# Last layer of a four-layer network: grouped norm shifts, a reordered spread, four identity sums and row-tiled FFN matmuls

## The chip, the cores and the metric

One core of a Trainium2 chip runs the kernel. The metric is the device time of one execution in microseconds (us), the median of several runs. Engines are named as in the profile: PE is TensorE's matmuls, PEld its weight loads, DVE is VectorE, ACT is ScalarE, POOL is GpSimd, SP is SyncE, which issues the DMAs.

## The reference

The input is x of shape (4, 32, 16, 16): 4 images, 32 channels, 256 pixels. Four layers run one after another, each as `x = x + layer(group_norm(x))`: a 7x7 dynamic filter, a deformable 3x3 convolution, twenty row and column updates, and the last layer, the only one that the change touches:

```
# last layer, x normalised, patches = 9 reflected 3x3 shifts of x
counts  = 1 + round(7 * (df - dmin) / (dmax - dmin + 1e-8))   # df = |laplacian(mean_c x)|
kvals   = minimum(counts, 9)
sim     = <x, patch_k> / (|x| * |patch_k|)                    # 9 per pixel
order   = argsort(-sim);  wts = exp(sim) where rank < kvals, else 0
out     = sum_k wts_k * patch_k / sum_k wts_k
enhanced = out + group_norm(x, weight, bias, 16 groups)
h       = relu(w1 @ enhanced + b1)                            # 32 -> 64 channels
return enhanced + w2 @ h + b2                                 # 64 -> 32 channels
```

## The kernel before

Partition 32b+c holds channel c of image b, so a tile is 128 partitions x 256 pixels. There is no loop over tiles: everything is written out by hand, and each engine runs its own list in order, with semaphores between them. `HALVES` are pixels 0 to 127 and 128 to 255. PSUM is one tensor `ps` of 8 banks x 512 floats. The last layer starts when the third layer's result is turned back (L1023 to L1031) and `x3` is made (L752).

**Norms and similarities.** ACT copies the normalised image to `g3c` (L555) and squares it into `maps[0]` (L557). PE makes the channel means (L1069), the squared norms of 324 padded pixels by one matmul with a 4-column weight (L1073), the Laplacian (L1078), and four maps of shifted dot products (L1084). ACT copies the norms three times, for the three column shifts, to `norms0`, all on partitions 0 to 3 (L562). PE transposes 3 column shifts x 3 row shifts x 2 halves of them, 18 transposes of 4 x 128 (L1093). ACT copies the dots (L565) and then takes the square root of the transposed norms (L567). DVE makes reciprocals of the norm products and `sim` (L786 to L802), and compares (L806, L808).

**Counts and ranks.** After the Laplacian DVE finds its largest and smallest value (L776 to L783). POOL makes the counts in three instructions, L439, L440 and L441, the last of which writes `kn` in bf16. PE adds up the ranks in bank 6: a constant (L1118), 16 matmuls of the comparisons (L1111), and two of `kn`, in bf16 (L1128). DVE turns rank and `exp(sim)` into weights `wf` (L821). `keep_warm` (L862) puts matmuls of zeros into PE's list, with counts from `WARM`.

**Spread and sum.** PE transposes `wf` (L1135), ACT and DVE copy it to `wrows`. `spread3(c)` (L1138) copies the weights of one column shift c to all channels: three matmuls of 32 rows, each into its own bank. DVE multiplies with the patches, three at a time (L837), giving `prod3[c]`, `prod3[3+c]`, `prod3[6+c]`. The third spread reuses the banks of the first, so it waits for the first product. The inverse weight sums `rden` are turned (L1157), copied (L576), spread (L1161) and copied to `rb` (L578). Six matmuls with the identity add the terms in bank 0 (L1167): some are products, some are pairs that POOL (L452) or DVE (L841) has added before.

**FFN.** `wc` holds w1 and w2 as block matrices of 128 x 128, two for each layer. Blocks off the pairs are zero. `normed` (L1148) puts w1 times the group-normed image into the hidden banks, L1189 adds w1 times `enh` (L845). ACT and DVE make the ReLU (L581, L849), L1194 multiplies with w2, accumulating two blocks, L854 adds bias and residual, and SP stores each half (L350). f32 matmuls are two records each in the profile, f32 transposes one.

POOL's list also has a stretch of fills and constant building (L414 to L429), between the second layer and its part of the third layer's moves, which wait for `g2` (L431 to L435).

Of the kernel before, what the change touches and what calls it, by code (L numbers as in the profile page):

```python
# [19 lines left out]
BF16 = mybir.dt.bfloat16  # L20
ALU = mybir.AluOpType
ACT = mybir.ActivationFunctionType
# [3 lines left out]
P = B * C  # L26
# [46 lines left out]
WARM = (9, 23, 12, 14, 5, 1, 2)  # L73
# [18 lines left out]

SHIFTS = (1, PAD - 1, PAD, PAD + 1)
# [23 lines left out]
def build(nc, x_d, par_d, ident_d, taps_d, wconv_d, wa_d, wb_d, wc_d, cst_d, sel_d, sel0_d, cb_d, out_d):  # L117
    with ExitStack() as ctx:
# [71 lines left out]
        norms0 = sb("norms0", [B, 3, PAD * W])  # L190
# [6 lines left out]
        kn = sb("kn", [B, HW], BF16)  # L197
# [9 lines left out]
        rden = sb("rden", [P, LINES, Q])  # L207
        wrows = sb("wrows", [P, HW])
        rrows = sb("rrows", [P, HW])
        rb = sb("rb", [P, HW])  # L210
        sum3 = sb("sum3", [P, 3, HW])
# [142 lines left out]
        def _(g):  # L354
# [104 lines left out]
        def _(a):  # L459
# [107 lines left out]
            a.activation(nn[:, :, :, :].rearrange("p l k b -> p (l k b)"), ps[:, 0, 0:LINES * KB],  # L567
                         ACT.Sqrt).then_inc(nn_ready, 1)
# [7 lines left out]
            a.activation(rrows[3 * Q:P, :], ps[3 * Q:P, 1, HW:2 * HW], ACT.Copy).then_inc(rrows_ready, 1)  # L576
            a.wait_ge(r_spread, 1)
            a.activation(rb[:, :], ps[:, 1, 0:HW], ACT.Copy).then_inc(rb_ready, 1)  # L578
            for n, pixels in enumerate(HALVES):
                a.wait_ge(h_done, 2 * n + 1)  # L580
# [4 lines left out]
        def _(v):  # L585
# [210 lines left out]
            v.tensor_tensor(some_k(sim, 4, 1), view(ps[:, 0, 4 * B:4 * B + 1], (KB, LINES), (B, 1), (1, B)),  # L796
# [7 lines left out]
            v.wait_ge(fills_ready, 3)  # L804
# [28 lines left out]
            v.reciprocal(rden[:, :, 0:B], den[:, :].rearrange("p (l b) -> p l b", b=B)).then_inc(rden_ready, 1)  # L833
# [7 lines left out]
            v.tensor_tensor(sum3[:, 2, :], prod3[:, 5, :], prod3[:, 8, :], ALU.add).then_inc(sum_v, 1)  # L841
# [461 lines left out]
```

## Time and profile before

| | us |
|---|---|
| median of 3 runs | 110.9 |
| lowest, highest | 110.66, 111.75 |
| profiled execution, its device time | 111.37 |
| its span, first to last instruction | 109.3 |
| PE busy in the span | 95.5 |
| DVE busy | 71.8 |
| ACT busy | 52.0 |
| POOL busy | 29.4 |

The span is 2.1 us shorter than the execution's time; what lies around it is start and end of the program. The profile page gives busy times, the clock granted to TensorE, and the chain of work that ended last. The timeline gives instructions in order of time, with the idle time of their engine before them and what ended it. Matmuls are pipelined, so their busy times overlap and start-to-start distances say more. Times in the text are from the span's start.

### The profile page before, as it was taken

What the parts mean: (1) busy time and instruction counts of PE and PEld (TensorE: products, weight loads), DVE (VectorE), ACT (ScalarE), POOL (GpSimd) and SP (SyncE); (2) the same over time, 40 slices, a digit from 0 to 9 for tenths busy, and PEclk for the clock granted to TensorE, in tenths of its full rate; (3) what the DMA queues carried; (4) which work ended last, traced back from release to release, by engine and by line L of the source; (5) the groups of instructions that cost most, each with busy time, mean ns of one, the idle gap of its engine ahead of it and who ended that gap; (6) DMA issues with size and microseconds to landing.
All of it is one profiled execution on the core that took longest, in us unless ns stands there. A gap on an engine that the chain in (4) does not pass through costs nothing.

```text
span 109.3 us, 2956 instructions
## 1 busy us (share of the span) xinstructions
PE 95.5 (87%) x1209; PEld 68.8 (63%) x1213; DVE 71.8 (66%) x201; ACT 52.0 (48%) x107; POOL 29.4 (27%) x43
## 2 busy tenths in 40 slices
PE   5959997596775999999967999999999899888990
PEld 2336642394555777777732899979998644554990
DVE  4653988139999998398437655565555669667542
ACT  5643826215999999757424999000000045621120
POOL 3000821790000003999972000000000000763130
PEclk9999999999999999999999999999999999999999
DMA  2899999999100000000000000000000000000001
GB/s 72 212 342 375 196 188 199 193 191 219 31 0 0 6 0 3 0 6 0 6 13 0 0 0 6 0 6 0 6 0 6 0 3 6 0 0 0 0 0 48
DMA packets 4684, 6.37 MB, mean 58 GB/s; under 512 B 560, under 2 KB 3936, under 8 KB 4672
## 3 DMA queue, kind: packets, MB, share of 16 engines
q1 hardware_dynamic: 4672, 6.20, 25.0%
q8 instruction: 9, 0.15, 0.6%
q14 instruction: 3, 0.02, 0.1%
HBM read 6.07 MB, written 0.13 MB: 57 GB/s over the span
## 4 chain that ended last, share of the span: by engine, by line
PE 69%; DVE 16%; ACT 5%; DMA 4%; issue 2%; SPq 1%; DVEq 0%
PE ps L1055 22%; PE ps L982 13%; PE ps L993 8%; PE ps L882 5%; DMA taps<-in_taps 4%; PE ps L862 3%; DVE st L698 3%; PE ps L1167 3%; PE ps L934 2%; DVE g1x L660 2%; DVE yt L734 2%; PE ps L919 1%; ACT s L532 1%; PE ps L1141 1%; PE ps L1189 1%
## 5 line engine op out<-in xcount | busy, mean ns | idle before, releaser
L698 DVE TENSOR_TENSOR st<-hats 128x1024 f32<-128x1024 f32 (+1 forms) x21 | 20.9, 1043 | 2.2 <-PE ps L982 2.2
L982 PE MATMUL ps<-ident,st 128*128 128x128 f32 x144 | 17.9, 277 | 2.4 <-DVE st L698 2.4
L532 ACT ACTIVATE s<-ps 128x512 f32<-128x512 f32 x33 | 17.3, 601 | 4.5 <-PE ps L982 4.5
L982 PEld LDWEIGHTS ps<-ident,st 128*128 128x128 f32 x144 | 15.6, 141 | 6.0 <-DVE st L698 3.5
L862 PE MATMUL ps<-zeros 128*128 128x512 bf16 x62 | 16.3, 409 | 2.4 <-DVE zeros L607 1.2
L1055 PE MATMUL ps<-yt,wband 128*64 128x96 f32 (+1 forms) x240 | 12.5, 260 | 0.8 <-DVE yt L734 0.8
L463 ACT ACTIVATE std<-mv,par 128x1 f32<-128x1 f32 x4 | 1.2, 295 | 24.6 <-DVE mv L595 24.6
L862 PEld LDWEIGHTS ps<-zeros 128*128 128x128 bf16 x66 | 6.6, 105 | 9.9 <-issue 1.9
L1055 PEld LDWEIGHTS ps<-yt,wband 128*64 128x64 f32 x240 | 11.5, 136 | 2.2 <-issue 1.2
L1055 PE MATMUL ps<-ytb,wband 128*64 128x96 f32 (+1 forms) x240 | 12.2, 259 | 0.1
L1055 PEld LDWEIGHTS ps<-ytb,wband 128*64 128x64 f32 x240 | 11.3, 136 | 0.9 <-DVE ytb L748 0.2
L741 DVE SCALAR_TENSOR_TENSOR ytb<-ps,ytb 128x64 f32<-128x64 f32 (+7 forms) x36 | 6.9, 228 | 5.4 <-PE ps L1055 5.4
L741 DVE SCALAR_TENSOR_TENSOR yt<-ps,yt 128x64 f32<-128x64 f32 (+7 forms) x36 | 6.9, 228 | 5.3 <-PE ps L1055 5.3
L993 PE MATMUL ps<-s,mixed 128*32 128x256 f32 x144 | 9.5, 385 | 0.9 <-ACT s L532 0.9
L439 POOL TENSOR_SCALAR df<-df,mm 4x256 f32<-4x256 f32 x1 | 1.2, 1220 | 33.6 <-DVE mm L783 33.6
L400 POOL TENSOR_TENSOR st<-hats 128x1024 f32<-128x1024 f32 x1 | 2.9, 2947 | 18.3 <-PE ps L982 18.3
L882 PE MATMUL ps<-taps,g0t 128*128 128x352 f32 (+1 forms) x20 | 5.9, 433 | 1.3 <-DMA taps<-in_taps 1.3
L410 POOL TENSOR_SCALAR wband<-wband 128x384 f32<-128x384 f32 x4 | 6.8, 1732 | 0.2 <-POOL st L400 0.2
L548 ACT ACTIVATE wband<-wband 128x384 f32<-128x384 f32 x16 | 6.7, 508 | 0.0
L993 PEld LDWEIGHTS ps<-s,mixed 128*32 128x32 f32 x144 | 3.8, 109 | 4.1 <-ACT s L532 1.1
L882 PEld LDWEIGHTS ps<-taps,g0t 128*128 128x128 f32 x20 | 3.5, 190 | 3.1 <-issue 1.8
L488 ACT ACTIVATE hid<-ps 128x512 f32<-128x512 f32 x4 | 2.2, 598 | 3.3 <-PE ps L893 3.3
(180 smaller groups left out, 128.8 us busy)
## 6 DMA issues: line engine op xcount, KB each, us to landing
wband<-in_wb SPq DMA_DIRECT2D x4, 720.0 KB, 15.8
wa<-in_wa SPq DMA_DIRECT2D x1, 576.0 KB, 8.3
taps<-in_taps SPq DMA_DIRECT2D x1, 560.0 KB, 5.9
taps<-in_taps SPq DMA_DIRECT2D x1, 448.0 KB, 4.8
wa<-in_wa SPq DMA_DIRECT2D x1, 324.0 KB, 5.8
wc<-in_wc SPq DMA_DIRECT2D x1, 256.0 KB, 14.9
cst<-in_cst SPq DMA_DIRECT2D x1, 242.0 KB, 6.1
sel<-in_sel SPq DMA_DIRECT2D x1, 192.0 KB, 5.0
```

The lines of the kernel that those rows point to most:

```text
L400: g.tensor_tensor(st[:, k % 2, half, :, :].rearrange("p b (y x) -> p b y x", x=W), view(hats[:, half, k, 0, 0:1], (16, B), (1, H), (0, W)) ...
L410: g.tensor_scalar(wband[:, n, :, :], wband[:, n, :, :], 2.0, None, ALU.mult).then_inc(early_doubled, 1)
L532: a.activation(s[:, k % 2, kb, 2 * pair:2 * pair + 2, :], ps[:, turn_bank(e), :], ACT.Copy).then_inc(drained_a, 1)
L548: a.mul(wband[:, n, :, :], wband[:, n, :, :], 2.0).then_inc(band_doubled, 1)
L698: v.tensor_tensor(st[:, k % 2, half, low:low + count, :].rearrange("p b (y x) -> p b y x", x=W), view(hats[:, half, k, low, 0:1], (16, cou ...
L741: v.scalar_tensor_tensor(out=lanes, in0=view(ps[:, Z_BANKS[n >= STEPS // 2][pair], frm:frm + 1], (H, 8), (1, count)), scalar=0.0, in1=lane ...
L862: t.matmul(ps[:, bank, :], zeros[:, 0:P], zeros[:, :], start=True, stop=True)
L882: last = t.matmul(out[:, :, y0:y0 + ROWS7, :], g0t[:, half, :], taps7[:, 2 * i:2 * i + n, lo:lo + ROWS7, :], start=(half == 0), stop=(half ...
L982: last = t.transpose(ps[:, turn_bank(e), HW * i + P * half:HW * i + P * half + P], st[:, k % 2, half, 2 * pair + i, P * kb:P * kb + P], id ...
L993: last = t.matmul(ps[Q * b:Q * b + Q, 0, 0:HW], mixed[:, kb, col:col + C], s[:, k % 2, kb, b, :], start=(k == 0 and kb == 0), stop=(k == T ...
L1055: last = t.matmul(ps[low:low + 64, Z_BANKS[n >= STEPS // 2][pair], 0:2 * LANE].rearrange("p (b n) -> p b n", b=2)[:, :, H * to:H * (to + c ...
L1167: return t.matmul(ps[:, 0, 0:HW], ident[:, :], term, start=first, stop=last)
```

## The change

It touches only the last layer and POOL's fills for it.

- The norms' weight becomes `norm3`, 96 columns wide, so that the squared norms come out on partitions 0 to 3, 32 to 35 and 64 to 67, and each column shift goes to a group of its own. Six transposes of 68 x 128 take the place of 18 of 4 x 128. The square root reads 12 of each 68 columns.
- POOL fills `norms0` and `norm3`, makes three small copies and `neg`, and no longer fills `rden`.
- `kn` is f32, and its matmul uses `neg`, in f32 too. The constant of the ranks (L1118) moves ahead of the `keep_warm` in front of the comparisons, behind a wait for `mm_ready`.
- One matmul of zeros fewer before the spreads. The wait for `lapw_ready` moves ahead.
- `rden` is turned by two transposes onto partitions 0 to 3. `spread3(2)` is issued ahead of the wait for `rrows` and the spread of the inverse sums.
- The sums: POOL adds a third (`sum3[1] + prod3[7]`), DVE a second (`prod3[2] + prod3[5]`, then `+ prod3[8]`). Four identity matmuls remain of six.
- FFN: each 128 x 128 matmul pair becomes four matmuls on the nonzero blocks, 32 rows x 64 columns for w1, 64 rows x 32 columns for w2.

```diff
-WARM = (9, 23, 12, 14, 5, 1, 2)
+WARM = (9, 23, 12, 14, 5, 1, 1)
+NT_ROWS = 2 * Q + B
...
# POOL
-            g.memset(rden[:, :, :], 0.0).then_inc(fills_ready, 1)
             g.memset(sim[:, LINES * KB:], 0.0).then_inc(fills_ready, 1)
+            g.memset(norms0[:, :], 0.0).then_inc(fills_ready, 1)
+            step(g.memset(norm3[:, :], 0.0))
+            for dx in range(3):
+                g.tensor_copy(norm3[:, Q * dx:Q * dx + B], cst[:, C_NORM:C_NORM + B]).then_inc(fills_ready, 1)
             step(g.memset(lapw[:, :], 0.0))
             g.wait_ge(ident_loaded, 16)
+            g.wait_ge(fills_ready, 6)
+            step(g.tensor_scalar(neg[:, :], ident[0:B, 0:B], -1.0, None, ALU.mult))
...
+            g.wait_ge(sum_g, 2)
+            g.tensor_tensor(sum3[:, 3, :], sum3[:, 1, :], prod3[:, 7, :], ALU.add).then_inc(sum_g, 1)
# ACT
             for dx in range(3):
-                a.activation(norms0[:, dx, :].rearrange("p (h w) -> p h w", w=W),
-                             view(ps[0:B, 7, dx:dx + 1], (PAD, PAD), (1, W)), ACT.Copy).then_inc(norms0_ready, 1)
+                group = slice(Q * dx, Q * dx + B)
+                a.activation(norms0[group, :].rearrange("p (h w) -> p h w", w=W),
+                             view(ps[group, 7, dx:dx + 1], (PAD, PAD), (1, W)), ACT.Copy).then_inc(norms0_ready, 1)
...
-            a.activation(rrows[3 * Q:P, :], ps[3 * Q:P, 1, HW:2 * HW], ACT.Copy).then_inc(rrows_ready, 1)
+            a.activation(rrows[:, :], ps[0:B, 1, HW:2 * HW], ACT.Copy).then_inc(rrows_ready, 1)
...
# DVE
-            v.tensor_tensor(sum3[:, 2, :], prod3[:, 5, :], prod3[:, 8, :], ALU.add).then_inc(sum_v, 1)
+            v.tensor_tensor(sum3[:, 4, :], prod3[:, 2, :], prod3[:, 5, :], ALU.add).then_inc(sum_v, 1)
+            v.wait_ge(sum_v, 1)
+            v.tensor_tensor(sum3[:, 2, :], sum3[:, 4, :], prod3[:, 8, :], ALU.add).then_inc(sum_v, 1)
...
# PE
-            t.matmul(ps[0:B, 7, 0:PAD * PAD], cst[:, C_NORM:C_NORM + B], maps[:, 0, :], start=True,
+            t.matmul(ps[0:3 * Q, 7, 0:PAD * PAD], norm3[:, :], maps[:, 0, :], start=True,
...
-            for dx in range(3):
-                t.wait_ge(norms0_ready, dx + 1)
+            t.wait_ge(norms0_ready, 3)
+            for half in range(2):
                 for dy in range(3):
-                    for half in range(2):
-                        at, frm = KB * half + B * (3 * dy + dx), P * half + W * dy
-                        last = t.transpose(ps[:, 0, at:at + B], norms0[:, dx, frm:frm + P], ident[0:B, 0:B])
+                    at, frm = NT_ROWS * (3 * half + dy), P * half + W * dy
+                    last = t.transpose(ps[:, 0, at:at + NT_ROWS], norms0[0:NT_ROWS, frm:frm + P],
+                                       ident[0:NT_ROWS, 0:NT_ROWS])
...
-                                view(cb[0:B, CB_NEG:CB_NEG + 1], (0, KNN), (1, B)),
+                                view(neg[:, 0:1], (0, KNN), (1, B)),
...
+            def hidden(n, image, first):
+                for b in range(B):
+                    i, j = b // 2, b % 2
+                    last = t.matmul(ps[64 * j:64 * j + 64, H_BANKS[n][i], 0:P],
+                                    wc[C * b:C * b + C, P * i + 64 * j:P * i + 64 * j + 64], image[C * b:C * b + C, HALVES[n]],
+                                    start=first, stop=not first, skip_group_check=True)
+                return last
...
             for half in range(2):
-                last = t.matmul(ps[3 * Q:P, 1, HW + LINE * half:HW + LINE * half + LINE], rden[:, half, :],
-                                ident[:, :], start=True, stop=True)
+                last = t.transpose(ps[0:B, 1, HW + LINE * half:HW + LINE * half + LINE], rden[:, half, :], ident[:, :])
             last.then_inc(rden_turned, 1)
-            t.wait_ge(rrows_ready, 1)
-            t.matmul(ps[:, 1, 0:HW], sel[3 * Q:P, 0:P], rrows[3 * Q:P, :], start=True, stop=True).then_inc(r_spread, 1)
             t.wait_ge(p3_ready, 1)
             spread3(2)
+            t.wait_ge(rrows_ready, 1)
+            t.matmul(ps[:, 1, 0:HW], sel[0:B, 0:P], rrows[:, :], start=True, stop=True).then_inc(r_spread, 1)
...
             add3(sum3[:, 0, :])
+            t.wait_ge(gnout_ready, 1)
             t.wait_ge(p3_ready, 2)
-            add3(prod3[:, 7, :])
-            t.wait_ge(sum_g, 2)
-            add3(sum3[:, 1, :])
-            t.wait_ge(p3_ready, 3)
-            add3(prod3[:, 2, :])
...
+            hidden(0, gnout, True)
+            t.wait_ge(sum_g, 3)
+            add3(sum3[:, 3, :])
+            t.wait_ge(sum_v, 2)
             add3(sum3[:, 2, :], last=True).then_inc(acc3_done, 1)
             t.wait_ge(rb_ready, 1)
-            normed(1, 0)
-            normed(1, 1)
+            hidden(1, gnout, True)
             for n, pixels in enumerate(HALVES):
                 t.wait_ge(enh_ready, n + 1)
...
+                hidden(n, enh, False).then_inc(h_done, 1)
             for n, pixels in enumerate(HALVES):
...
+                t.wait_ge(h_a, n + 1)
+                t.wait_ge(h_v, n + 1)
+                for b in range(B):
+                    i, j = b // 2, b % 2
+                    last = t.matmul(ps[C * b:C * b + C, Y_BANKS[n], 0:P],
+                                    wc[64 * j:64 * j + 64, P * (2 + i) + C * b:P * (2 + i) + C * b + C],
+                                    hff[64 * j:64 * j + 64, i, pixels], start=True, stop=True)
                 last.then_inc(ffn_done, 1)
```

`H_BANKS` is ((5, 6), (7, 1)) and `Y_BANKS` is (2, 3), so in `hidden` two 32-row tiles write one bank, on different partitions, and in the last matmuls all four 64-row tiles write one bank, on different partitions.

## Rows read from the trace of the kernel before

**Rows 1.** The profile page: TensorE's granted clock, in 40 slices of the span

```profile
PEclk9999999999999999999999999999999999999999
```

**Rows 2.** Timeline, 89 to 94: start, duration, engine, line, out<-in, count, [idle before <-releaser]

```profile
89.80 0.61 PE L1069 MATMUL ps<-cst,g3c 128*128 128x4 f32 x4
...
90.34 0.71 PE L1073 MATMUL ps<-maps,cst 128*4 128x324 f32 x2
...
92.39 1.06 PEld L1093 LDWEIGHTS ps<-ident,norms 4*128 4x128 f32 x16 [0.86 <-ACT norms L562]
...
92.50 0.60 ACT L565 ACTIVATE dots<-ps 128x512 f32<-128x512 f32 x1 [0.43 <-PE ps L1084]
...
93.70 0.23 ACT L567 ACTIVATE nn<-ps 128x72 f32<-128x72 f32 x1 [0.61 <-PE ps L1093]
```

**Rows 3.** Timeline, 93 to 97: the counts on POOL, and the ranks

```profile
93.29 1.22 POOL L439 TENSOR_SCALAR df<-df,mm 4x256 f32<-4x256 f32 x1 [33.55 <-DVE mm L783]
...
94.59 0.40 POOL L440 TENSOR_SCALAR df<-df 4x256 f32<-4x256 f32 x1
95.07 1.06 POOL L441 TENSOR_SCALAR kn<-df 4x256 bf16<-4x256 f32 x1
...
96.01 0.20 PE L1118 MATMUL ps<-cb 1*128 1x72 bf16 x1 [0.69 <-DVE above L806]
...
96.64 0.21 PE L1128 MATMUL ps<-cb,kn 4*128 4x36 bf16 x2
...
96.96 0.30 DVE L821 SCALAR_TENSOR_TENSOR wf<-ps,ex 128x36 f32<-128x36 f32 x2 [0.54 <-PE ps L1128]
```

**Rows 4.** Timeline of POOL, 45 to 60

```profile
53.77 0.53 POOL L420 TENSOR_SCALAR lapw<-ident 128x128 f32<-128x128 f32 x1
...
59.12 0.62 POOL L435 COPY yt<-g 32x64 f32<-32x64 f32 x2 [2.14 <-DVE g L604]
```

**Rows 5.** Timeline of DVE, 56 to 58

```profile
56.64 0.63 DVE L725 TENSOR_TENSOR x<-x,r 128x256 f32<-128x256 f32 x1 [1.80 <-ACT r L535]
```

**Rows 6.** Timeline, 97.6 to 103: spreads, products, sums

```profile
97.68 0.29 DVE L826 COPY wrows<-ps 128x128 f32<-128x128 f32 x1 [0.43 <-PE ps L1135]
...
98.12 1.14 PE L1141 MATMUL ps<-wrows,sel 32*128 32x256 f32 x12
...
98.88 1.82 DVE L837 TENSOR_TENSOR prod<-ps,g3p 128x768 f32<-128x768 f32 x2 [0.42 <-PE ps L1141]
...
99.19 0.62 PE L1157 MATMUL ps<-ident,rden 128*32 128x128 f32 x4
...
99.91 1.59 POOL L452 TENSOR_TENSOR sum<-prod 128x256 f32<-128x256 f32 x2 [2.02 <-DVE prod L837]
...
101.09 0.96 DVE L837 TENSOR_TENSOR prod<-ps,g3p 128x768 f32<-128x768 f32 x1 [0.39 <-PE ps L1141]
...
102.08 0.42 DVE L841 TENSOR_TENSOR sum<-prod 128x256 f32<-128x256 f32 x1
```

**Rows 7.** The chain of waits in order of time, 101 to 104.3: start, us, what

```profile
101.00 2.35 PE ps L1167 x10
103.35 0.45 PE ps L1148 x4
103.80 0.43 PE ps L1167 x2
```

**Rows 8.** Timeline, 104.3 to the last store

```profile
104.34 0.49 DVE L845 TENSOR_TENSOR enh<-ps,rb 128x128 f32<-128x128 f32 x2 [1.83 <-PE ps L1167]
...
104.68 1.16 PE L1189 MATMUL ps<-enh,wc 128*128 128x128 f32 x8
...
105.68 1.11 PE L1194 MATMUL ps<-hff,wc 128*128 128x128 f32 x8
106.46 0.79 DVE L854 SCALAR_TENSOR_TENSOR y<-ps,par,xe 128x128 f32<-128x128 f32 x2 [0.23 <-PE ps L1194]
106.84 0.85 SPq L350 DMA_DIRECT2D out<-y  x2
```

More of the change, by code:

```diff
@@ L206, in build @@
         den = sb("den", [P, LINES * B])
-        rden = sb("rden", [P, LINES, Q])
+        rden = sb("rden", [P, LINES, B])
         wrows = sb("wrows", [P, HW])
-        rrows = sb("rrows", [P, HW])
+        rrows = sb("rrows", [B, HW])
         rb = sb("rb", [P, HW])
-        sum3 = sb("sum3", [P, 3, HW])
+        sum3 = sb("sum3", [P, 6, HW])
         gn = sb("gn", [P, 12])
@@ L566, in _ @@
             a.wait_ge(norms_turned, 1)
-            a.activation(nn[:, :, :, :].rearrange("p l k b -> p (l k b)"), ps[:, 0, 0:LINES * KB],
-                         ACT.Sqrt).then_inc(nn_ready, 1)
+            a.activation(nn[:, :, :, :].rearrange("p l (y x) b -> p (l y) x b", x=3),
+                         view(ps[:, 0, 0:1], (NT_ROWS, 3 * LINES), (Q, 3), (1, B)), ACT.Sqrt).then_inc(nn_ready, 1)
             a.wait_ge(gn_paired, 1)
@@ L832, in _ @@
             v.wait_ge(v_step, own[0])
-            v.reciprocal(rden[:, :, 0:B], den[:, :].rearrange("p (l b) -> p l b", b=B)).then_inc(rden_ready, 1)
+            v.reciprocal(rden[:, :, :], den[:, :].rearrange("p (l b) -> p l b", b=B)).then_inc(rden_ready, 1)
             for c in range(3):
@@ L1105, in _ @@
                      stop=True).then_inc(gn_paired, 1)
+            t.wait_ge(mm_ready, 1)
+            t.wait_ge(wc_loaded, 32)
+            t.matmul(view(ps[:, 6, 0:1], (KB, LINES), (B, KNN), (1, B)), cb[0:1, CB_ONE:CB_ONE + LINE],
+                     view(cb[0:1, CB_TAP:CB_TAP + 1], (0, LINES), (G, KNN), (1, B)),
+                     start=True, stop=False, skip_group_check=True)
             keep_warm(WARM[4], 1)
@@ L1116, in _ @@
             t.wait_ge(above_ready, 1)
-            t.wait_ge(wc_loaded, 32)
-            t.matmul(view(ps[:, 6, 0:1], (KB, LINES), (B, KNN), (1, B)), cb[0:1, CB_ONE:CB_ONE + LINE],
-                     view(cb[0:1, CB_TAP:CB_TAP + 1], (0, LINES), (G, KNN), (1, B)),
-                     start=True, stop=False, skip_group_check=True)
             for o in range(1, NEAR + 1):
@@ L1144, in spread3 @@
                 last.then_inc(wb_done, 1)
-            def normed(n, i):
-                t.matmul(ps[:, H_BANKS[n][i], 0:P], wc[:, P * i:P * i + P], gnout[:, HALVES[n]], start=True,
-                         stop=False, skip_group_check=True)
+            def hidden(n, image, first):
[5 more added lines that the diff above has]
+                return last
             t.wait_ge(sel_ready, 1)
@@ L1171, in _ @@
             add3(sum3[:, 0, :])
+            t.wait_ge(gnout_ready, 1)
             t.wait_ge(p3_ready, 2)
-            add3(prod3[:, 7, :])
-            t.wait_ge(sum_g, 2)
-            add3(sum3[:, 1, :])
-            t.wait_ge(p3_ready, 3)
-            add3(prod3[:, 2, :])
-            t.wait_ge(gnout_ready, 1)
-            normed(0, 0)
-            normed(0, 1)
-            t.wait_ge(sum_v, 1)
+            hidden(0, gnout, True)
+            t.wait_ge(sum_g, 3)
+            add3(sum3[:, 3, :])
+            t.wait_ge(sum_v, 2)
             add3(sum3[:, 2, :], last=True).then_inc(acc3_done, 1)
             t.wait_ge(rb_ready, 1)
-            normed(1, 0)
-            normed(1, 1)
+            hidden(1, gnout, True)
             for n, pixels in enumerate(HALVES):
                 t.wait_ge(enh_ready, n + 1)
-                for i in range(2):
-                    t.matmul(ps[:, H_BANKS[n][i], 0:P], wc[:, P * i:P * i + P], enh[:, pixels], start=False,
-                             stop=True, skip_group_check=True).then_inc(h_done, 1)
+                hidden(n, enh, False).then_inc(h_done, 1)
             for n, pixels in enumerate(HALVES):
-                for i, ready in ((0, h_a), (1, h_v)):
-                    t.wait_ge(ready, n + 1)
-                    last = t.matmul(ps[:, Y_BANKS[n], 0:P], wc[:, P * (2 + i):P * (3 + i)], hff[:, i, pixels],
-                                    start=(i == 0), stop=(i == 1))
+                t.wait_ge(h_a, n + 1)
[5 more added lines that the diff above has]
+                                    hff[64 * j:64 * j + 64, i, pixels], start=True, stop=True)
                 last.then_inc(ffn_done, 1)
```

16 lines of the change are left out of this document (9 added, 7 removed).

## The prediction

> **What bounds the kernel.** I read the page first, then the chain of waits in order of time, then the timeline of each engine over the last 25 us. The page shows TensorE's clock granted in full in all 40 slices [rows 1], so no term below needs a clock. The chain shows where the last layer's end is made. From 101.00 to 104.23 it is PE alone: ten records of identity matmuls, four of `normed`, two more identity records [rows 7]. DVE had its last sum ready at 102.50 [rows 6] and then waited 1.83 for PE [rows 8]. After that enh, hidden matmuls, ReLU, last matmuls and bias alternate to 107.25, and SP's second store goes out at about 107.28, half of its 0.85 before 107.69 [rows 8]. In front, two paths meet at the ranks: norms, similarities and comparisons, for which PE waited 0.69 [rows 3], and POOL's counts, ready at 95.07 + 1.06 = 96.13 [rows 3]. The second is only 0.5 ahead of the matmul that needs it, at 96.64. This decides what the first part of the change is worth.
>
> **Norms.** The 18 transposes are issued from 92.39; 16 of them make one piece of 1.06, some 0.066 each [rows 2]. Six at 0.07 to 0.11 end near 93.0, where the square root now starts at 93.70. But ACT is copying the dots until 92.50 + 0.60 = 93.10 [rows 2], so the root starts at about 93.12: 0.58 earlier, and so do reciprocals, `sim` and comparisons. The ACT copies keep their size and end before PE is free at 92.39; waiting for all three costs nothing. L1073 with 96 columns runs in the mode of L1069, and the change to 4-column tiles comes one step later, at L1078: I take +0.04 for the Laplacian and what hangs on it, between -0.1 and +0.2. Moving L1118 away takes its lead over the first rank matmul out, between 0 and its 0.20 [rows 3]; I take 0.13, as matmuls overlap. PE would be done with the 16 rank matmuls at 96.64 - 0.58 - 0.13 = 95.93 and could start `kn`.
>
> **Counts.** It can't, since `kn` is not there. What matters is whether an f32 output makes L441 quicker. L440 does the same 256 elements in 0.40, L441 in 1.06, L439 in 1.22 [rows 3]. L439 writes f32 as L440 does and is slow; L420 writes f32, 128 elements, in 0.53 [rows 4]. L440 multiplies and adds; the others subtract first, or multiply alone. So the slow ones go with the operation pair, not with the type, and I leave L441 at 1.06 (bounds 0.40 and 1.06). `kn` is ready at 96.13 + 0.04 = 96.17 and PE starts at about 96.22; a wait costs 0.05 to 0.07 (L452 starts 0.07 behind the first product's end at 98.88 + 0.96 [rows 6]). The matmul is now f32: four passes with 128-column weights and a short moving side, as L1069, 0.61 [rows 2], where bf16 took 0.21 [rows 3]. That ends at 96.83, against 96.85. The gain of 0.58 + 0.13 is worth 0.02 to 0.04 at L821. If L441 took 0.40, ranks would end at 95.93 + 0.61 = 96.54, 0.31 earlier.
>
> The Trainium skill, page GPSIMD Engine Reference, section Engine selection, says that one-input elementwise work on GpSimd is roughly at line rate. By it L441 should go at L440's pace; three rows here do not agree. By the page the sum would be 0.27 lower.
>
> **POOL's fills.** Two fills, three copies of 128x4 and one 4x4 multiply come in, one fill goes. Each copy at most 0.31 (half of L435), the others at most 0.53 (L420): below 2.1 with the fill that goes, and likelier 1.3 to 1.6. The idle time that covers them is 2.14, ended by `g2` [rows 4]; without the cover each 0.1 would cost 0.1 only once POOL's move came behind DVE's moves. Not quite free: POOL now works under DVE's stage around 57. L725 took 0.63 [rows 5] while POOL added too, the same form in L841 0.42 [rows 6]. I take +0.05 (-0.2 to +0.2).
>
> **Fewer zeros, third spread.** The first spread's matmul starts 0.15 behind the end of L826 [rows 6]; that is two waits rather than the zeros, so the dropped one is worth 0 (0 to 0.08). The turning of `rden`, now two single passes of four, still ends before the first product at 98.88 + 0.96 - 0.04 = 99.80. There the third spread starts, at 99.86, and needs 0.76 as the first did (98.12 to 98.88): third product at 100.62 and not 101.09, just when DVE is free of the second. DVE is 0.47 ahead, product done at 101.58. The inverse sums come behind it in the same rows of the array, ready in `rb` near 101.4, before anyone asks.
>
> **Sums.** DVE now makes two: 101.61 + 2 x 0.42 + 0.04 = 102.49, so what it was ahead is spent. POOL: 1.59 for two from 99.87, a wait of 0.08, another 0.73: 102.27. Both now read SBUF twice at the same time, as in L725: 0 to 0.4 more for DVE, 0 to 0.2 for POOL; I take 102.7 and 102.4. PE has two pairs of identity records done by 102.0 and `hidden` by 102.45. The last two pairs start at 102.5 and need 4 x 0.22 and a tail of 0.25: 103.63 where it was 104.23. **Gain 0.60** (0.45 to 0.75).
>
> **FFN in tiles.** From the first half of enh, 104.63, to the last y, 107.25, it is 2.62 now. The spread is the nearest row for tiles of 32 rows: 12 records in 1.14, where L1167 takes 2.35 for 10 of the same 256 columns [rows 6, 7]; three row tiles do run at once. With 128 columns I take 0.45 for a `hidden` and 0.45 for the last matmuls, mode changes included. First half: 0.05 + 0.45 + 0.04 + ReLU 0.37 + 0.05 + 0.45 + 0.12 + 0.35 = 1.88; second half 0.3 behind, 2.2 in all. The stores need 0.42 each on SP, so the second goes out 0.12 later than y would let it. **Gain 0.30** (0 if tiles take what the full matmuls take, 0.50 if they overlap fully). The second `hidden` of `gnout` lies under DVE's enh.
>
> **The sum.** 0.60 + 0.30 - 0.05 = 0.85. The profiled execution took 111.37, with a span of 109.3: that gives 110.5 and a span of 108.4. The median of the runs shown is 110.9; less 0.8, **110.1 us**. Own range of this case 109.7 to 110.6.
>
> **Rivals.**
> *The counts get fast* (0.15). L441 was slow through its bf16 output. L1128's start then hangs on the norms: another 0.27, 109.8 us. For it: L441 is the only one of the three with bf16. Against: L439 and L420.
>
> *Tiles don't pay* (0.13). Each `hidden` and each set of last matmuls costs as much as the full ones with their mode changes, 1.16 and 1.11 for two halves [rows 8]. FFN gain 0, and 0.1 less before the last adds: 110.5 us. The half of the change that shortens the FFN would do nothing.
>
> *Tiles in one bank go one after another* (0.12), the rival on the slow side. In the trace row tiles always write banks of their own (L1141: one bank for each of three), so no row excludes it. `hidden` would take 8 x 0.11 less half, +0.2 in three places on the path; the last matmuls, four tiles in one bank, 8 x 0.11 = 0.88 a half and not 0.22, +0.85 over both with their overlap gone: 110.1 + 1.4 = 111.5 us. It decides from half of this on; 0.85 lost is no change.
>
> The Trainium skill, page PSUM — Partial Sum Buffer, section PSUM bank collisions raise a hardware error, speaks against the change here: different row tiles can't access one PSUM bank at the same time, and software has to see to it. It also tells that different quadrants of one bank went clean for two engines. No row of this trace shows either.
>
> **Chances.** The rest, 0.60, is the forecast: counts bind, tiles run together. The range must hold forecast, fast counts and idle tiles: from 109.4 (all good bounds together reach 109.3) to 110.9. About 1% is what a measurement of this kernel can tell from no change, that is 109.8 and 112.0. Below 109.8 lie a quarter of the forecast and 0.7 of the fast counts: 0.26. Above 112.0, three in ten of the serial case and a little for contention nobody saw: 0.05. Within: 0.69.
>
> **What would show it.** Right: L567 at about 93.1; L441 still 1.06 and PE idle before L1128; L821 at 96.9; third L837 at 100.6 without idle time; last identity record ended by 103.7; y's last end 2.2 behind enh's first. Wrong: L441 near 0.4; L841 pairs beyond 1.3; records of `hidden` at 0.11 or more apart; POOL later than DVE at its moves for the third layer. Wrong altogether if the first 90 us differ by more than 0.3, since only fills were added there.

## The result and the profile after

The changed kernel takes 115.16 us (median of four executions, 114.63 to 115.75). The kernel before, in four executions beside it, took 111.33 (110.66 to 114.89). The ratio is 1.0366, with a 95% interval of 1.0268 to 1.0465. The ratios in this text compare only executions within 1.5% of the fastest of their own kernel, so the one of 114.89 is left out, while all four of the changed kernel count. The forecast was 110.1. The profiled execution took 115.49, its span is 113.2, and its mean granted clock is 0.94.

The page of the changed kernel, slices of a fortieth of the span (2.83 us) each:

```profile
span 113.2 us, 2980 instructions
...
PEclk9999999769999999999999999999999999955559
```

TensorE's clock was granted in full in every slice of before [rows 1]. Here it falls twice: for a while in slices 8 and 9, and for four slices in the last layer. The view by stretches of the same kernel gives the sizes (start:end and length, then busy time and instructions of PE, PEld, DVE, ACT and POOL, then the granted clock, the DMA share and GB/s):

```profile
21.10:24.60 3.50, 3.50 (x60) 3.50 (x62) 0.82 (x1) 0.34 (x1) 2.44 (x3) 0.51 1.09 191
86.00:99.50 13.50, 11.91 (x135) 6.58 (x136) 9.66 (x38) 5.34 (x13) 4.17 (x5) 1.00 0.01 2
99.50:110.00 10.50, 10.36 (x68) 5.87 (x66) 4.76 (x10) 1.34 (x4) 3.04 (x5) 0.51 0.00 0
110.00:113.20 3.20, 0.70 (x16) 0.19 (x10) 0.84 (x3) 0.15 (x1) 0.00 (x0) 1.00 0.14 41
```

From 99.5 to 110.0 the clock is at its lower level, 1.2 GHz, and that is all of spread and sums and the FFN up to its last matmuls, where PE sets the end. The chain of work that ended last in the changed kernel (start, length, engine and line, number of instructions), from the counts on:

```profile
94.23 1.35 POOL df L447
...
95.65 0.40 POOL df L448
...
96.13 1.16 POOL kn L449
...
97.33 0.63 PE ps L1142 x4
...
98.32 0.45 PE ps L1149 x2
...
99.23 1.73 PE ps L1155 x12
...
101.48 1.16 PE ps L1155 x6
...
103.48 2.01 PE ps L1184 x4
105.49 0.63 PE ps L1164 x8
106.13 2.01 PE ps L1184 x4
108.13 1.20 PE ps L1164 x16
```

L1155 is `spread3`, L1184 the identity sum, L1164 `hidden`. The eight identity records come in two groups of 2.01, about 0.50 each, where before had 0.23 [rows 7]. DVE and POOL, which set the time of the sums in the forecast, are nowhere in the chain between the spread and `hidden`.

**Where 4.12 us went.** The two profiled executions differ by 115.49 - 111.37 = 4.12. The last layer's zeros (L875; L862 before) start at 87.63 and not at 86.84: 0.79 came before it, with the early fall at 21.1. From there to the end of the last y it is 111.19 - 87.63 = 23.56 against 107.26 - 86.84 = 20.42, which is 3.14 more. What is left, 0.19, lies behind y and outside the span. So most of the loss lies where the clock was low, and the experiments ask first what the same code takes where it isn't.

### The profile page after: what moved, and what is told of

It reads as the page before. It is cut to its first block, busy times and chain, and to the rows that moved or that the text cites. A ratio compares the mean times of both kernels' runs of the same rounds, so it can differ in the third digit from the quotient of the medians.

```text
span 113.2 us, 2980 instructions
## 1 busy us (share of the span) xinstructions
PE 99.9 (88%) x1216; PEld 69.9 (62%) x1220; DVE 72.8 (64%) x202; ACT 52.1 (46%) x107; POOL 31.3 (28%) x49
## 4 chain that ended last, share of the span: by engine, by line
PE 68%; DVE 14%; ACT 6%; DMA 4%; issue 3%; POOL 3%; SPq 1%; DVEq 0%
PE ps L1068 21%; PE ps L995 12%; PE ps L1006 8%; PE ps L895 5%; PE ps L947 4%; PE ps L1184 4%; DMA taps<-in_taps 4%; DVE st L709 3%; PE ps L875 3%; PE ps L1155 3%; DVE g1x L671 2%; PE ps L1164 2%; ACT yt L554 1%; PE ps L932 1%; ACT s L542 1%
## 5 line engine op out<-in xcount | busy, mean ns | idle before, releaser
L875 PE MATMUL ps<-zeros 128*128 128x512 bf16 x61 | 15.9, 407 | 2.5 <-DVE zeros L618 1.2
L875 PEld LDWEIGHTS ps<-zeros 128*128 128x128 bf16 x65 | 6.3, 103 | 9.9 <-issue 1.9
L947 PE MATMUL ps<-wa,a1x 128*64 128x72 f32 x72 | 4.1, 306 | 0.7 <-ACT a1x L509 0.7
```

Source lines behind the costliest of these rows:

```text
L875: t.matmul(ps[:, bank, :], zeros[:, 0:P], zeros[:, :], start=True, stop=True)
L947: last = t.matmul(ps[low:low + 64, 7, OFFS * half:OFFS * half + OFFS], a1x[:, dx, at + low:at + low + 64], wa[:, col:col + OFFS], start=(d ...
```

## Experiments: the clock

Line numbers in the profiles are each kernel's own. Executions of the kernel before stood beside each; over the three series, each on another chip, there were 71. Only one execution of a run has a trace. What the others did is told by their mean granted clock and their time. By these the clock fell near the end in 19 of the 71 (mean clock under 0.96, 114.67 to 116.15 us): 6 of 25, 7 of 20 and 6 of 26. In 8 it fell only early (mean 0.983 or 0.984, 111.5 to 112.5), and the median of those that kept it is 110.63. "Fell" below means a fall near the end; how many there were is told for each kernel.

**One matmul of zeros given back.** The changed kernel, with one edit:

```diff
-WARM = (9, 23, 12, 14, 5, 1, 1)
+WARM = (9, 23, 12, 14, 5, 1, 2)
```

> The changed kernel with the one matmul of zeros back in front of the spreads. Theory 'zeros': the dropped matmul is what lets TensorE's clock fall to half at 98.9 us in the changed kernel's trace; then the clock stays at 1.0 to the end and the time is 110 to 111 us. Theory 'thin stretch': PE has had too little to do over several us (6 transposes for 18, waits for the counts), one matmul of 0.2 us does not mend it: clock still 0.94 to 0.95, time 114.5 to 115.5. Theory 'late waits' (POOL's contention and the counts cost the time, not the clock): 115 as well, but with a stretch from the ranks to the end as long as now whatever the clock does.

Measured: median 111.11 of ten executions, one of which fell (115.93). Ratio 1.0067 (1.0027 to 1.0106). The profiled execution took 110.66 with a span of 108.2. Its page:

```profile
PEclk9999999999999999999999999999999999999998
```

And its chain, from the matmul of `kn` on:

```profile
95.82 0.63 PE ps L1142 x4
...
96.81 0.44 PE ps L1149 x2
97.24 0.43 PE ps L875 x2
...
97.72 0.73 PE ps L1155 x6
```

The two zeros matmuls (L875 x2) end 0.05 before the spread, which had to wait for `wrows` anyway, and its first six records take 0.73. From the zeros at 86.06 to the end of the last y at 106.03 this is 19.97, against 20.42 before and 23.56 in the changed kernel. So the new work is 0.45 quicker than the old at full clock, and the fall costs 23.56 - 19.97 = 3.59. One matmul that costs nothing by its own time separates four falls in four from one in ten.

**Four more zeros.** The changed kernel with `WARM` at `(9, 23, 12, 14, 6, 2, 2)`, which is three more, and a fourth ahead of the wait for `kn`:

```diff
...
+            keep_warm(1, 1)
...
```

> The changed kernel with four more matmuls of zeros in places where PE waits: one more before the comparisons, one before the wait for kn, one more after the ranks, one more before the spreads. Theory 'thin stretch': the clock holds at 1.0 from the third layer to the end; time 110.0 to 111.5 us. Theory 'zeros' also gives that. Theory 'late waits': no better than 115, since PE's waits get longer, not shorter. If tiles in one bank went one after another, the FFN from the first enh to the last y would still take over 3.5 us at full clock; if they run together, 2.2.

Measured: 111.10, none of ten fell, ratio 1.0055 (1.0014 to 1.0097). Together with the run before it: where the clock is kept, the changed kernel gains nothing over before; it is 0.6% slower. The sections below ask why.

**The same edit in the kernel before.** Only the last number of `WARM`, from 2 to 1:

```diff
-WARM = (9, 23, 12, 14, 5, 1, 2)
+WARM = (9, 23, 12, 14, 5, 1, 1)
```

> The kernel before with only the one matmul of zeros taken away. Theory 'zeros': the clock falls near 99 us here too, time 114 to 115. Theory 'thin stretch': little happens, 110.9 within 0.5, clock 1.0 in most executions.

Measured: 7 of 10 fell (113.45 to 115.27), median 113.71. The three that kept the clock have a median of 110.45 (ratio 0.9988, 0.9933 to 1.0042), so no change is seen there. The kernel before fell in 6 of the 25 executions beside it, and in 19 of all 71. So dropping the matmul makes falls more frequent by itself, with none of the new work around it. Whether it does so less often than in the changed kernel, four and ten executions can't tell. The time it takes is nothing; a fall that it holds off is worth some 4 us.

**The zeros put elsewhere.** The changed kernel, with the extra one in front of the comparisons and not before the spread:

```diff
-WARM = (9, 23, 12, 14, 5, 1, 1)
+WARM = (9, 23, 12, 14, 6, 1, 1)
```

> The changed kernel with one more matmul of zeros, but ahead of the comparisons instead of in front of the spreads (6, 1, 1 for 5, 1, 1). Theory 'amount': how much PE has done over the stretch decides, wherever it is done: clock falls in few executions, as with the zeros back in their place (1 of 10), median near 111.1. Theory 'place': only work in the last stretch before the spreads holds the clock: falls in most executions, median 114 to 115.5.

Measured: three of four fell, median 115.21 (111.27 to 115.96). So far as four executions can tell, one more in the earlier gap doesn't make up for the one that is missing ahead of the spread.

**Full FFN matmuls.** The changed kernel with `hidden` and the last matmuls as before, 128 x 128:

```diff
...
-            hidden(0, gnout, True)
+            normed(0, 0)
+            normed(0, 1)
...
-                hidden(n, enh, False).then_inc(h_done, 1)
+                for i in range(2):
+                    t.matmul(ps[:, H_BANKS[n][i], 0:P], wc[:, P * i:P * i + P], enh[:, pixels], start=False,
+                             stop=True, skip_group_check=True).then_inc(h_done, 1)
```

> The changed kernel with the FFN of before (full 128 x 128 matmuls), all else as changed. If the light tiles of the FFN are what keeps the clock down for 10 us, the clock comes back sooner and the time is under 114. Theory 'thin stretch': the fall at about 99 us is ahead of the FFN, so it stays; with full matmuls at half clock the time is 115 to 117, clock 0.94 to 0.95.

Measured: four of four fell, 115.14. Since all did, its ratio of 1.0386 (1.0316 to 1.0456) holds the fall. The clock was low from 98.5 to 108.7. The light tiles are not what lets it fall.

**What PE did before the fall.** The same 13.5 us, counted from 1.63 before the last layer's zeros, in five kernels. The changed kernel's is the row 86.00:99.50 above. The kernel before:

```profile
85.21:98.71 13.50, 12.32 (x152) 7.15 (x153) 9.32 (x38) 5.23 (x13) 3.96 (x5) 1.00 0.01 2
```

With one given back:

```profile
84.43:97.93 13.50, 12.08 (x136) 6.64 (x137) 9.66 (x38) 5.34 (x13) 4.22 (x5) 1.00 0.01 2
```

Two kernels of the next section, the norms alone, and the last version, with two more zeros and the constant moved:

```profile
85.22:98.72 13.50, 11.96 (x140) 6.57 (x141) 9.79 (x38) 5.35 (x13) 4.23 (x5) 1.00 0.01 2
...
85.13:98.63 13.50, 12.88 (x154) 7.54 (x155) 9.34 (x38) 5.22 (x13) 3.96 (x5) 1.00 0.01 2
```

PE is busy for 11.91 where four of four fell, but for 11.96 in the norms alone, where none of ten did. Then come 12.08 for one of ten, 12.32 for 19 of 71, and 12.88 for none of ten. So how much PE does in these 13.5 us doesn't order the kernels. What orders them better is the number of zeros matmuls right ahead of the spread:

| ahead of the spread | executions that fell |
|---|---|
| one | 4 of 4, 4 of 4 (full FFN), 3 of 4 (moved), 7 of 10 (before, one dropped): 18 of 22 |
| two | 19 of 71 (before), and 11 of 78 in nine kernels of these experiments: 30 of 149 |

Where the fall begins differs too. Five traces hold one near the end, each 10.2 long. In the three with one such matmul it begins 11.8 to 12.0 behind the last layer's zeros (99.6 in the changed kernel), in the spread. In the two that have the norms and ranks of before (the tiles alone and the six fills, both below) it begins 9.2 and 8.9 behind them, at the end of PE's wait ahead of the ranks or within it. The wait in the tiles alone, whose clock is low from 95.9 on:

```profile
95.89 0.24 PE L1118 MATMUL ps<-cb 1*128 1x72 bf16 x1 [0.69 <-DVE above L806]
```

The zeros ahead of the spread come only after that place (97.48 in before, 10.64 behind the last layer's zeros), so they can't hold off a fall there. That fits two weak places, of which the change and the dropped matmul bear on the second; no run shows it by itself. The kernel before keeps or loses the clock with one and the same list, so what decides in a single execution isn't shown either.

The Trainium skill, page TensorE: Matmul & The Clock Gate, section A second HAM failure mode: psum-queue depth-cycling, tells of a kernel in which the engine idles shortly but often between groups of matmuls, and the clock goes up and down between its two levels. The trace agrees in part: the fall at 99.6 comes behind 1.6 us of idle time (13.50 - 11.91) in short pieces, none of them over 0.3. But the norms alone have 1.5 there and kept the clock in ten of ten, and before has 1.2, with one piece of 0.69 [rows 3], and mostly keeps it.

## Experiments: the parts, at a clock that stays

**Norms alone.** The kernel before with the norms in three groups, the fills for them, and the wait for `lapw_ready` moved; `kn` stays bf16 and the constant of the ranks stays in its place:

```diff
...
-            for dx in range(3):
-                t.wait_ge(norms0_ready, dx + 1)
+            t.wait_ge(norms0_ready, 3)
+            for half in range(2):
                 for dy in range(3):
-                    for half in range(2):
-                        at, frm = KB * half + B * (3 * dy + dx), P * half + W * dy
-                        last = t.transpose(ps[:, 0, at:at + B], norms0[:, dx, frm:frm + P], ident[0:B, 0:B])
+                    at, frm = NT_ROWS * (3 * half + dy), P * half + W * dy
+                    last = t.transpose(ps[:, 0, at:at + NT_ROWS], norms0[0:NT_ROWS, frm:frm + P],
+                                       ident[0:NT_ROWS, 0:NT_ROWS])
...
```

> The kernel before with only the norms part of the change: 96-column weight, three partition groups, 6 transposes of 68 rows for 18, and POOL's fills for it; kn stays bf16, the constant of the ranks stays where it was. Theory 'the counts bind': the similarities come about 0.55 us earlier but POOL's three count instructions end the wait, so the ranks end within 0.1 of before, or 0.2 to 0.4 later if POOL and DVE now disturb each other (a count instruction of 1.2 to 1.3 where it was 1.06); at full clock 110.7 to 111.1. Theory 'norms were the bound': 110.2. A second question, where the 0.5 us more between span and execution time of the changed kernel come from: if from POOL's fills or the norms, it shows here as 2.3 instead of 1.8.

Measured: 111.12, none of ten fell, ratio 1.000 (0.996 to 1.004). POOL's timeline of this kernel (start, length; in brackets the idle time before and its releaser):

```profile
93.45 1.25 POOL L448 TENSOR_SCALAR df<-df,mm 4x256 f32<-4x256 f32 x1 [33.71 <-DVE mm L793]
94.78 0.40 POOL L449 TENSOR_SCALAR df<-df 4x256 f32<-4x256 f32 x1
95.26 1.30 POOL L450 TENSOR_SCALAR kn<-df 4x256 bf16<-4x256 f32 x1
```

And DVE's, in the same kernel:

```profile
93.63 0.47 DVE L797 TENSOR_TENSOR pr<-nc_ 128x72 f32<-128x72 f32 x1
...
95.17 0.46 DVE L816 TENSOR_TENSOR above<-sim 128x288 bf16<-128x288 f32 x1
95.55 0.48 DVE L818 TENSOR_TENSOR above<-sim 128x128 bf16<-128x128 f32 x1
...
96.93 0.30 DVE L831 SCALAR_TENSOR_TENSOR wf<-ps,ex 128x36 f32<-128x36 f32 x2 [0.63 <-PE ps L1138]
```

The norms are early as forecast: `pr` starts 0.18 behind POOL's first instruction of the counts, before 0.90 behind. Three things are seen. The third instruction of the counts (L450 here, L441 before) takes 1.30 and not 1.06, with `kn` in bf16, so the output type is not what makes it slow. `pr` takes 0.47 for 0.23, and the second comparison 0.48 for 0.28; the first stays at 0.46. And PE waits for `kn`, which ends at 95.26 + 1.30 = 96.56; the weights `wf` start at 96.93, before at 96.96. The counts bind, and of the 0.58 only 0.03 is left.

The Trainium skill, page GPSIMD Engine Reference, section 1. Specifications, says that GpSimd shares its SBUF interfaces with VectorE, with contention when a VectorE instruction has two SBUF inputs. The trace agrees in kind: `pr` and the comparisons have two such inputs, and `pr`, the second comparison and POOL's third instruction got slower. It also shows that running side by side isn't enough: before, `pr` lies under the end of POOL's first instruction (94.19 to 94.42 of 93.29 to 94.51) and takes 0.23, and both comparisons start beside L441. What in the new order costs the time isn't shown.

**Spread and sums alone.** The kernel before with `rden` on four partitions, the third spread ahead of the inverse sums, and four identity sums:

```diff
...
-            v.tensor_tensor(sum3[:, 2, :], prod3[:, 5, :], prod3[:, 8, :], ALU.add).then_inc(sum_v, 1)
+            v.tensor_tensor(sum3[:, 4, :], prod3[:, 2, :], prod3[:, 5, :], ALU.add).then_inc(sum_v, 1)
+            v.wait_ge(sum_v, 1)
+            v.tensor_tensor(sum3[:, 2, :], sum3[:, 4, :], prod3[:, 8, :], ALU.add).then_inc(sum_v, 1)
...
```

> The kernel before with only the earlier third spread, the two transposes of the inverse sums and the four identity sums; FFN and norms as before. The prediction's gain at the last identity record: 0.60 at full clock, so 110.1. Theory 'POOL's third sum takes it back': 0.3 to 0.45, 110.4. Execution minus span 1.8, if the 0.5 comes from the norms part.

Measured: 110.50, one of ten fell, ratio 0.9976 (0.9927 to 1.0026). DVE's timeline of this kernel:

```profile
98.60 2.74 DVE L838 TENSOR_TENSOR prod<-ps,g3p 128x768 f32<-128x768 f32 x3 [0.42 <-PE ps L1144]
101.37 0.94 DVE L842 TENSOR_TENSOR sum<-prod 128x256 f32<-128x256 f32 x1
102.35 0.42 DVE L844 TENSOR_TENSOR sum<-sum,prod 128x256 f32<-128x256 f32 x1
103.63 0.49 DVE L848 TENSOR_TENSOR enh<-ps,rb 128x128 f32<-128x128 f32 x2 [0.86 <-PE ps L1169]
```

Three products run without a gap, 2.74 in all, as forecast. The first sum takes 0.94 where the same form right behind it takes 0.42. From the spread's start (97.85) to `enh` it is 5.78; before it was 104.34 - 98.12 = 6.22. The gain in the trace is 0.44. That is 0.4% of the execution. The ratio's interval holds it, and holds no gain as well.

**FFN in tiles alone.** The kernel before with `hidden` and the tiled last matmuls:

```diff
...
+            def hidden(n, image, first):
...
+                for b in range(B):
+                    i, j = b // 2, b % 2
+                    last = t.matmul(ps[64 * j:64 * j + 64, H_BANKS[n][i], 0:P],
+                                    wc[C * b:C * b + C, P * i + 64 * j:P * i + 64 * j + 64], image[C * b:C * b + C, HALVES[n]],
+                                    start=first, stop=not first, skip_group_check=True)
...
```

> The kernel before with only the FFN in tiles. Tiles run together: 0.3 to 0.4 off from the first enh to the last y, 110.3 to 110.5 at full clock. Tiles in one bank one after another: 0.8 or more on top, 111.5. If light tiles let the clock fall, executions at clock 0.93 to 0.96 are more than the 6 of 25 of the kernel before.

Measured: 110.75, 112.68, 113.54 and 114.86. The last is the profiled one, and fell. Of the other three, two have 3.5 and 3.7 us outside the span, so the times say nothing of 0.3 us. The page of the one that fell:

```profile
span 113.1 us, 3006 instructions
...
PEclk9999999999999999999999999999999999555799
```

The clock was low from 95.9 to 106.1. That begins before the spread, and so before the first tile. The tiles' own size is read where the clock stays, in the changed kernel with one zeros matmul given back. Its timeline of all engines:

```profile
103.32 0.45 PE L1164 MATMUL ps<-gnout,wc 32*64 32x128 f32 x8
...
103.85 0.67 PE L1164 MATMUL ps<-enh,wc 32*64 32x128 f32 x16
...
104.86 0.68 PE L1206 MATMUL ps<-hff,wc 64*32 64x128 f32 x16 [0.35 <-ACT hff L592]
105.42 0.61 DVE L867 SCALAR_TENSOR_TENSOR y<-ps,par,xe 128x128 f32<-128x128 f32 x2 [0.45 <-PE ps L1206]
105.80 0.85 SPq L353 DMA_DIRECT2D out<-y  x2
```

Sixteen records of `hidden` take 0.67 and sixteen of the last matmuls 0.68, over both halves; eight full ones took 1.16 and 1.11 [rows 8]. `hidden` has two row tiles a bank, on 64 partitions each, and the last matmuls have four tiles in one bank, on 32 each. They run together: four records of `hidden` start within 0.02 of each other (103.85 to 103.87) and last 0.32 each, the next four follow at 104.01. From `enh` at 103.50 to the end of y it is 2.53, before 107.26 - 104.34 = 2.92: 0.39 less.

**Both together.** Sums and tiles in the kernel before:

```diff
...
+            g.tensor_tensor(sum3[:, 3, :], sum3[:, 1, :], prod3[:, 7, :], ALU.add).then_inc(sum_g, 1)
...
+            hidden(0, gnout, True)
...
```

> The kernel before with the spread, sums and FFN parts, without the norms and counts part, and with both matmuls of zeros in front of the spreads. If the parts add up: 0.45 + 0.40 less 0.12 for the stores, 110.0 at full clock, and clock falls no more often than in the kernel before.

Measured: five of ten fell, median 113.03; the lowest was 109.96 with a span of 108.2. Ratio where the clock stayed 0.997 (0.9911 to 1.003).

**With zeros against the fall.** The same with two more matmuls of zeros ahead of the comparisons:

```diff
-WARM = (9, 23, 12, 14, 5, 1, 2)
+WARM = (9, 23, 12, 14, 7, 1, 2)
```

> Spread, sums and FFN parts on the kernel before, with 7 matmuls of zeros instead of 5 ahead of the comparisons, where PE waited 0.69 us. Without them 5 of 10 executions fell. Theory 'amount': at most 2 of 10 fall, median 110.0 to 110.6, faster than the kernel before by 0.3 to 0.8. Theory 'light tiles let the clock fall': still about half of them, median 111 to 115.

Measured: none of ten fell, 111.07 (109.68 to 112.67), ratio 1.0013 (0.9964 to 1.0061).

**And the constant of the ranks moved,** as the changed kernel has it, ahead of these zeros:

```diff
+            t.wait_ge(mm_ready, 1)
+            t.wait_ge(wc_loaded, 32)
+            t.matmul(view(ps[:, 6, 0:1], (KB, LINES), (B, KNN), (1, B)), cb[0:1, CB_ONE:CB_ONE + LINE],
...
-            t.wait_ge(wc_loaded, 32)
-            t.matmul(view(ps[:, 6, 0:1], (KB, LINES), (B, KNN), (1, B)), cb[0:1, CB_ONE:CB_ONE + LINE],
```

> As the last one, and the constant of the ranks ahead of the zeros, as in the change. The first rank matmul starts 0.13 earlier and the counts (ready at 96.1) are not yet the bound, so 0.1 less than the last one at full clock: 109.9 to 110.4.

Measured: none of ten fell, 110.65 (110.03 to 111.38), ratio 0.9981 (0.9936 to 1.0027). In the profiled executions the last layer, from zeros to y, takes 19.48, 0.94 less than before, and the median span where the clock stayed is 108.2 against 108.7 in the kernel before beside it. The execution shows little of that: in four of ten 2.4 to 2.9 us lie outside the span and not 1.8. Why is open. At a clock that stays, this version is not shown to be quicker than before. Over all executions its mean is lower, 110.68 against 111.96, since none of ten fell and 19 of 71 did. But a kernel that falls as often as before would come through ten executions without a fall in about one case of twenty (0.73 to the tenth is 0.04), so ten are few to call the gain shown.

**Six small fills on POOL.** The ratio of 1.0067 wanted a cause, since the changed kernel with one zeros matmul given back has the shorter span where the clock stays (median 108.6, before 108.8). The kernel before with six fills of 16 columns of a tile that nobody reads:

```diff
...
+            for n in range(6):
+                g.memset(spare[:, 16 * n:16 * n + 16], 0.0)
```

> The kernel before with six small fills of an unused tile in POOL's list, nothing else. Question: the changed kernel's execution is 2.2 to 2.5 us longer than its span, the kernel before 1.8, the norms part alone 2.1. If POOL's longer list does it, this one shows 2.0 to 2.3 and 111.0 at full clock. If not, 1.8 and 110.7; then it lies in what the norms part puts on PE or ACT.

Measured: three of four fell, median 115.51; the one that kept its clock took 110.64 with a span of 108.4. What counts here is the time outside the span, execution minus span:

| kernel | POOL instructions | outside the span, median us |
|---|---|---|
| before | 43 | 1.81 |
| before, one zeros dropped | 43 | 1.77 |
| sums alone | 43 | 1.82 |
| both together | 43 | 1.81 |
| both, with two more zeros | 43 | 1.85 |
| both, and the constant moved | 43 | 1.92 |
| norms alone | 48 | 2.11 |
| six fills | 49 | 2.24 |
| full FFN matmuls | 49 | 2.25 |
| changed kernel | 49 | 2.27 |
| the zeros put elsewhere | 49 | 2.36 |
| four more zeros | 49 | 2.40 |
| one zeros given back | 49 | 2.45 |

Left out are the four executions of the tiles alone, which don't agree (1.76, 2.05, 3.54, 3.68). Six instructions that do nothing for the result add 0.43, and all four executions lie from 2.23 to 2.28. The changed kernel has six more too, and 0.46 more. With one zeros matmul given back it is 2.45 - 1.81 = 0.64 more, of which the count of POOL's instructions leaves 0.18 unexplained. Its gain in the span of 0.2 is lost there, and some 0.4 with it; the medians at a kept clock differ by 0.46 (111.09 and 110.63). Single executions with 43 instructions reach 2.4 to 3.7 as well, so POOL's list is one cause of several.

## Why the prediction was wrong

115.16 lies above the range of 109.4 to 110.9, and on the other side of before. Two steps failed, three terms were mis-sized, and one place was not looked at. The two steps are about TensorE's clock and carry nearly all of the miss.

**"TensorE's clock granted in full in all 40 slices, so no term below needs a clock."** This step failed, and carries the 3.59. The page is one execution: it tells what one execution of that list was granted. Over 71 executions the same list lost the clock in 19. The changed list was another one, and the range had no case for a low clock. The times before gave no sign (110.66 to 111.75 in three); `keep_warm`, a function that only keeps PE busy, did.

**"The dropped one is worth 0 (0 to 0.08)".** Right in its own time, wrong as a price. By itself this edit brought the kernel before from 19 in 71 to 7 in 10, and taking it back brought the changed kernel from four in four to one in ten.

**Norms, 0.58 earlier.** Right: from the last layer's zeros to `nn` it is 6.29, before 6.86, so 0.57.

**Counts, a gain of 0.02 to 0.04.** The mechanism was right, in that `kn` comes last and PE waits 0.16 for it; two sizes were off. POOL's timeline of the changed kernel with one zeros matmul given back:

```profile
92.66 1.24 POOL L447 TENSOR_SCALAR df<-df,mm 4x256 f32<-4x256 f32 x1 [33.71 <-DVE mm L794]
93.99 0.39 POOL L448 TENSOR_SCALAR df<-df 4x256 f32<-4x256 f32 x1
94.46 1.30 POOL L449 TENSOR_SCALAR kn<-df 4x256 f32<-4x256 f32 x1
```

And its PE:

```profile
94.90 0.76 PE L1129 MATMUL ps<-above,cb 128*128 128x64 bf16 x16 [0.34 <-DVE above L817]
95.82 0.63 PE L1142 MATMUL ps<-neg,kn 4*128 4x36 f32 x4 [0.16 <-POOL kn L449]
```

L449, taken at 1.06, is 1.30 (+0.24), with DVE's instructions in another place beside it. The Laplacian, taken at +0.04, comes 4.19 behind the zeros, before 4.05, so +0.14. So `kn`'s matmul starts 9.76 behind the zeros, before 9.80: a gain of 0.04 where 0.42 was forecast (96.64 - 96.22). Its f32 form takes 0.63, as forecast, and not 0.21. The forecast gain was to pay for that and didn't; since an f32 `kn` makes the counts no quicker, this 0.42 buys nothing. Together the spread starts 97.72 - 86.06 = 11.66 behind the zeros, before 98.12 - 86.84 = 11.28: 0.38 lost where a small gain was forecast.

**Rival "the counts get fast".** Refuted: L449 writes f32 in 1.30 (1.15 in the changed kernel's own trace), and the norms alone, with bf16, show 1.30 too.

**Spread and third product.** Right, also its cause: three products without idle time.

**Sums, gain 0.60 (0.45 to 0.75).** 0.44. The step that was mis-sized is "0 to 0.4 more for DVE, 0 to 0.2 for POOL". In the changed kernel with the clock kept, DVE's timeline shows all of it on one instruction:

```profile
101.24 0.94 DVE L852 TENSOR_TENSOR sum<-prod 128x256 f32<-128x256 f32 x1
102.22 0.42 DVE L854 TENSOR_TENSOR sum<-sum,prod 128x256 f32<-128x256 f32 x1
```

The first, beside POOL's last sum (0.72 from 101.18), takes 0.52 more; POOL loses nothing. In the changed kernel's own trace POOL's ends at 103.58 and DVE's starts at 103.69, and there it takes 0.42. DVE's last sum is ready 102.64 - 97.72 = 4.92 behind the spread's start, where the forecast had 102.7 - 98.12 = 4.58: 0.34 late. PE's weight loads idle 0.17 and 0.41 before the last identity matmuls.

**FFN tiles, gain 0.30.** Right: 0.39 up to the last y, forecast 2.62 - 2.2 = 0.42, and behind y 0.13 is given back to the stores, where 0.12 was forecast. The rivals "tiles don't pay" and "tiles in one bank go one after another" are refuted by the records above. The Trainium skill, page PSUM — Partial Sum Buffer, section PSUM bank collisions raise a hardware error, says that different row tiles can't access one bank at the same time. The trace doesn't agree for these tiles, which write one bank, each to partitions of its own: they ran together.

**The sum.** In the last layer, at a kept clock, it is +0.38 - 0.44 - 0.39 = -0.45, as the two traces have it; the forecast had 0.85 to the end of the execution. Outside the span +0.4 to +0.6 comes on top, for which the prediction had nothing: it costed the fills only by what covered them in the span. There its +0.05 was about right: L725's form takes 0.72 in the changed kernel, before 0.63 [rows 5], and from its start to the last layer's zeros it is 87.63 - 57.33 = 30.30, before 86.84 - 56.64 = 30.20.

**"Wrong altogether if the first 90 us differ by more than 0.3."** They differed by 0.79 in the profiled executions, of which 0.10 goes with the fills and the rest comes with an early fall at 21.1, ahead of every instruction that was edited. By the mean clock before has such a fall too, in 8 of 71 by itself. In the eleven kept traces without one, each of another kernel, the last layer's zeros start anywhere from 86.06 to 86.85, so 0.3 was too narrow for this sign. The early fall is not shown to be of the change.

**What stays open.** Why one and the same kernel keeps its clock in one execution and not in the next; whether a fall ahead of the ranks and one in the spread are two cases; whether sums or tiles raise the share (five of ten together, one of ten for the sums, too few to tell); whether POOL's fills do (three of four); by which way POOL's instructions lengthen the execution outside the span, and what else does.

## What to carry to other kernels

A page that shows the clock in full for one execution is no proof of a margin: look at all executions for a second group some per cent up, and if a kernel has matmuls of zeros, count each of them as a bet on the clock (3.6 us here), not as its own 0.2 us. Where it stands matters: the one ahead of the spread helped, one more in an earlier gap did not. After a change to PE's list, try one more matmul of zeros before the change itself is judged. And a chain that finishes 0.57 early gains nothing while another one binds behind it: the counts were ready no earlier, and they, `pr` and a comparison got longer as the two engines' work came to lie in another order.

## What the runs showed of the hardware

- One 512-column matmul of zeros ahead of the spread separates four falls in four from one in ten. In five traces a fall near the end lasts 10.2 us (99.6 to 109.9 in the changed kernel), at 1.2 GHz and not 2.4. In the changed kernel PE was never idle for over 0.3 at a time in the 13.5 us before it.
- Six POOL fills of 16 columns lengthen the execution by 0.43 outside the span, 0.07 each. The one execution that kept its clock has a span of 108.4, no longer than before's.
- DVE's add of two SBUF tiles of 128 x 256 takes 0.42 alone and 0.94 beside POOL's add of the same size. `pr` takes 0.47 when it starts 0.18 behind POOL's first count, and 0.23 when it starts 0.90 behind. In the changed kernel's own trace it keeps 0.23 at 0.17 behind, and POOL's instruction takes 1.34 for 1.24.
- Tiles of `hidden`, two to a bank: 16 records of 128 columns in 0.67, where 8 full ones take 1.16. Tiles of the last matmuls, four to a bank: 16 in 0.68, where 8 take 1.11.
